# Edge messages of a graph network on one core: 42-wide one-hots, three accumulated row products, another order of steps, another beginning and close

## The chip, the cores and the metric

The kernel runs on one NeuronCore of a Trainium2 chip. The metric is device time in microseconds. Five engines work side by side, each through its own list in order, and wait for each other through semaphores: TensorE (PE), VectorE (DVE), ScalarE (ACT), GpSimd (POOL) and SyncE (SP), which here only starts transfers.

## The reference

A graph of 3125 nodes with 32 features each and 53125 edges (sorted by destination) goes through one layer. For every edge the features of its source and its destination are gathered, a small network of the edge's ten numbers gives weights, and the products are summed per edge; the edge outputs are summed over each destination, added to the features, and normalised.

```python
xs, xd = (x[edge_src], x[edge_dst])
s1 = concatenate([xs[:, :8], xd[:, :8]]); v1 = concatenate([xs[:, 8:], xd[:, 8:]])
w = _mlp(emb, fc1_w1, fc1_w2)            # E x 512
s_t = a1 * (einsum('eu,euw->ew', s1, Wss) + einsum('eu,euw->ew', vdot1, Wvv))
v_t = a1 * (einsum(s1, Wsv) * sh1 + einsum('euk,euw->ewk', v1, Wvs))
w2 = _mlp(emb, fc2_w1, fc2_w2)           # E x 384
edge_out = concatenate([tanh(scal), vecs * tanh(gates)]) * norm
x = _layernorm(x + segment_sum(edge_out, edge_dst, 3125))
```

## The kernel before

The edges lie in 104 blocks (`NB`) of 512 (`BE`), four tiles of 128 each. A block's destinations lie within 42 (`WIN`) consecutive nodes, counted from a base per block.

Every engine runs the same loop over `STEPS`, from -5 to 106. In step i an engine works on several blocks at once: step i has the main products of block i, the first layer of block i+1, the turned features of block i+2, the destination rows of block i+3, the turned one-hot of block i+4, and the late work (gates, tanh, sums over nodes) of blocks i-1 to i-3. The order of the work is that of the calls in each engine's loop, written by hand; nothing else schedules it.

For a block, in the order of its life:

- POOL gathers the sources' rows into `xs` by four indirect transfers (`gather`, L311), two blocks ahead of their use.
- DVE makes the one-hot of the destinations (`one_hot`, L520), bf16. It is 126 wide: 42 places, three times over, since the features `x` are stored in DRAM as three bf16 parts whose sum is the float32 value. PE turns it with four transposes (`turn_one_hot`, L708) and ACT copies the result to `oht` (`copy_oht`, L410).
- SP loads the block's 42 rows of all three parts into `window`, 126 partitions (`load_window`, L247). PE multiplies `oht` by `window` (`rows`, L752): four products, each contracting over 126 rows at once, so that the three parts are summed inside one product. ACT copies the rows into `fe` (`copy_rows`, L435).
- POOL makes the directed features from `fe` (`directions`, L351 to L357). PE turns `fe` (`turn_features`, L715), ACT copies it to `f` (`copy_f`, L416).
- PE makes the two hidden layers (`hidden`, L773 and L774) and multiplies `f` by the first weights (`first_layer`, L782). DVE multiplies by the hidden layer (`products`, L580), PE repeats and sums (`repeat`, L740), DVE multiplies again (`products2`, L603), PE sums (`sum_2`, L724) and turns (`turn`, L762), DVE and ACT make the outputs, PE sums them over the block's nodes (`over_nodes`, L732), DVE adds them to `acc`.

A wait that matters below: `rows(m)` waits until `copy_f` of block m-1 is done, for both use bank 4 of PSUM; ACT's list has `copy_oht` ahead of `copy_f`. `first_layer(m)` waits for both of DVE's instructions of `products2(m-1)`.

Before the loop stands the beginning: all inputs are loaded, `x` is split in three parts and stored to DRAM (`x_dram`), the first twelve blocks of edge attributes likewise (`e_dram`), the directions `r4` of all edges are normalised on DVE in one go, the constants and weights are made, and `acc` is zeroed on POOL. After the loop stands the close: the nodes' own features are multiplied by a centring matrix (L827) and the sums likewise (L833), and the norm is taken.

Of the kernel before, what the change touches and what calls it, by code (L numbers as in the profile page):

```python
# [7 lines left out]
BF16 = mybir.dt.bfloat16  # L8
# [7 lines left out]
D = 32  # L16
# [8 lines left out]
WK = PARTS * WIN  # L25
# [7 lines left out]
CHUNK = 32 * NT  # L33
HALVES = ((0, 13), (13, NT))
# [8 lines left out]
def program(nc, xp, xt, src_t, dst_t, base_t, bases_row, emb, vec_t, wgt, w1, w2a, w2b, out):  # L43
    ctx = ExitStack()
    with ctx:
# [9 lines left out]
        ones = sb("ones", [128, 1])  # L55
        iota_i = sb("iota_i", [128, P], I32)
        iota = sb("iota", [128, P])
        rank_i = sb("rank_i", [128, PARTS, WIN], I32)
        rank = sb("rank", [128, WK], BF16)
# [6 lines left out]
        no_rows = sb("no_rows", [WIN, PARTS, D], BF16)  # L66
# [13 lines left out]
        x_dram = nc.dram_tensor("x_dram", (PARTS, N + WIN, D), BF16, kind="Internal").ap()  # L80
# [3 lines left out]
        window_r = [sb(f"window{n}", [WK, D], BF16) for n in range(3)]  # L84
        oh_r = [sb(f"oh{n}", [128, T, WK], BF16) for n in range(OH)]
        oht_r = [sb(f"oht{n}", [WK, BE], BF16) for n in range(2)]
# [34 lines left out]
        x_part = early(P, PARTS * NT * D // 2).bitcast(BF16).rearrange("p (n m c) -> p n m c", n=PARTS, m=NT)  # L121
# [29 lines left out]
        oht_ps = ps[0:WK, 6, :].bitcast(BF16)[:, 0:BE]  # L151
# [17 lines left out]
        misfits_ready = sem("misfits_ready")  # L169
        n2_ready = sem("n2_ready")  # L170
        norm_ready = sem("norm_ready")
# [70 lines left out]
        def _(sp):  # L242
            def load_window(m):
# [3 lines left out]
                sp.dma_start(window_r[m % 3][:], x_dram[:, bass.ds(base, WIN), :]).then_inc(window_loaded[m % 3], 16)  # L247
# [21 lines left out]
            sp.dma_start(src_i[:], src_t).then_inc(src_loaded, 16)  # L269
            sp.dma_start(xt_s, xp.rearrange("(p m) c -> p m c", p=P)).then_inc(xt_loaded, 16)  # L270
            sp.dma_start(dst_i[:], dst_t).then_inc(dst_loaded, 16)
            sp.dma_start(base_i[:], base_t).then_inc(dst_loaded, 16)
            sp.dma_start(bases[:], bases_row).then_inc(bases_loaded, 16)
            load_super(0)
            sp.wait_ge(zeroed, 1)
            sp.dma_start(x_dram[:, N:N + WIN, :].rearrange("n m c -> m n c"), no_rows[:]).then_inc(x_stored, 16)
            for n in range(PARTS):
                sp.wait_ge(x_part_ready, n + 1)
                sp.dma_start(x_dram[n, 0:N, :].rearrange("(p m) c -> p m c", p=P), x_part[:, n, :, :]).then_inc(x_stored, 16)
            sp.wait_ge(bases_loaded, 16)  # L280
            sp.wait_ge(x_stored, 64)
# [608 lines left out]
```

## Time and profile before

| | us |
|---|---|
| median of three runs | 899.51 (896.36 to 900.3) |
| the profiled execution | 897.27 |
| its span | 895.4 |
| PE busy | 793.5 (89%) |
| DVE busy | 737.8 (82%) |
| POOL busy | 593.1 (66%) |
| ACT busy | 382.9 (43%) |

The profile's own execution is 1.87 us longer than its span, and 2.24 us shorter than the median. Busy time is an average over the whole span. What sets the pace is read from the order of time inside one step: who starts when, and who waited for whom. The timeline's rows give start, length, engine, line and operation; in brackets stands how long the engine was idle before, and what ended that. A row with xN merges N instructions: its length reaches from the first start to the last end. Ends of matmuls are modelled, starts are recorded; so the distance between two starts on PE is the safer number. A float32 product is two records on PE.

### The profile page before, as it was taken

The numbers are of one execution on the slowest core, as the hardware profiler recorded it, in microseconds if no ns is written. First come the engines' busy times: TensorE is split into PE (matmuls) and PEld (weight loads), VectorE is DVE, ScalarE is ACT, GpSimd is POOL, SyncE is SP. The second block draws the span as 40 slices with busy tenths as digits, with TensorE's granted clock in tenths as the row PEclk, the third lists the DMA queues.
The fourth block names the chain that finished last, engine by engine and source line by source line (L and its number), as shares of the span: only waits on it lengthen the run. The fifth ranks groups of instructions, "written<-read, shape, count | busy, mean of one in ns | idle before, by whom it ended". The sixth has DMA issues, their size and how long they took to land.

```text
span 895.4 us, 16890 instructions
## 1 busy us (share of the span) xinstructions
PE 793.5 (89%) x5234; PEld 362.1 (40%) x5234; DVE 737.8 (82%) x1397; ACT 382.9 (43%) x965; POOL 593.1 (66%) x866
## 2 busy tenths in 40 slices
PE   0179999999999999999999999999999999999983
PEld 0134444444444444444444444444444444444430
DVE  5648888888888888888888888888888888888873
ACT  3134444444445444444444444444454444444421
POOL 4877766677667667776677666767676667766300
PEclk9999999999999999999999999999999999999996
DMA  5111101111111111010111111111110110100000
GB/s 146 41 32 23 39 21 28 28 40 22 23 32 27 34 24 34 22 38 21 34 23 40 23 31 22 39 24 22 34 36 22 23 30 22 36 21 21 17 1 18
DMA packets 43733, 27.10 MB, mean 30 GB/s; under 512 B 21852, under 2 KB 42221, under 8 KB 43642
## 3 DMA queue, kind: packets, MB, share of 16 engines
q1 hardware_dynamic: 29498, 17.64, 7.5%
q0 software_dynamic: 13312, 6.84, 4.4%
q10 hardware_dynamic: 832, 1.52, 0.6%
q8 instruction: 42, 0.69, 0.3%
q14 instruction: 49, 0.40, 0.1%
HBM read 21.77 MB, written 4.20 MB: 29 GB/s over the span
## 4 chain that ended last, share of the span: by engine, by line
PE 78%; ACT 8%; issue 7%; DVE 3%; DMA 1%; POOL 1%; SPq 0%; ACTq 0%; DVEq 0%; POOLq 0%
PE ps L740 40%; PE ps L782 13%; PE ps L724 10%; PE ps L762 7%; ACT f L416 7%; PE ps L752 3%; PE ps L708 3%; PE ps L732 3%; DMA e_in<-in_emb 1%; DVE z_s L603 0%; POOL xs L311 0%; DVE w_f L569 0%; ACT oht L410 0%; PE ps L827 0%; PE ps L833 0%
## 5 line engine op out<-in xcount | busy, mean ns | idle before, releaser
L311 POOL DMA_INDIRECT xs<-in_xp,src_i x416 | 398.6, 958 | 110.4 <-issue 95.6
L740 PE MATMUL ps<-p_s,rep_m 128*128 128x512 f32 x832 | 374.5, 593 | 1.7 <-DVE p_s L580 1.7
L580 DVE TENSOR_TENSOR p_s<-ps,h 128x1024 f32<-128x1024 f32 x208 | 244.9, 1219 | 75.7 <-PE ps L782 75.7
L603 DVE TENSOR_TENSOR z_s<-ps,h 128x1024 f32<-128x1024 f32 x208 | 253.5, 1219 | 50.4 <-PE ps L740 50.2
L740 PEld LDWEIGHTS ps<-p_s,rep_m 128*128 128x128 f32 x832 | 150.0, 190 | 153.4 <-issue 149.2
L351 POOL TENSOR_TENSOR along<-fe,r 128x192 f32<-128x192 f32 x104 | 53.5, 514 | 127.1 <-issue 121.1
L410 ACT COPY oht<-ps 126x512 bf16<-126x512 bf16 x104 | 60.9, 586 | 177.6 <-PE ps L708 177.6
L422 ACT COPY u<-ps 128x512 f32<-128x512 f32 x104 | 61.0, 587 | 146.8 <-PE ps L724 146.8
L782 PE MATMUL ps<-f,w_f 32*128 32x512 f32 x832 | 119.5, 644 | 1.3 <-DVE z_s L603 1.3
L724 PE MATMUL ps<-z_s,w_z 128*32 128x512 f32 x832 | 108.0, 591 | 0.0
L404 ACT ACTIVATE eo_all<-gsc 128x64 f32<-128x64 f32 x104 | 26.7, 256 | 146.4 <-DVE gsc L618 144.9
L762 PEld LDWEIGHTS ps<-ident,u 128*128 128x128 f32 x416 | 43.8, 142 | 86.4 <-issue 86.3
L520 DVE TENSOR_TENSOR oh<-rank,place 128x504 bf16<-128x504 bf16 x104 | 70.1, 677 | 0.1
L708 PEld LDWEIGHTS ps<-ident_h,oh 128*126 128x126 bf16 x416 | 40.7, 140 | 70.2 <-issue 68.6
L715 PE MATMUL ps<-ident,fe 128*128 128x128 f32 x416 | 64.0, 277 | 5.1 <-POOL fe L357 5.1
L762 PE MATMUL ps<-ident,u 128*128 128x128 f32 x416 | 68.4, 287 | 0.0
L416 ACT COPY f<-ps 128x512 f32<-128x512 f32 x104 | 61.5, 591 | 9.7 <-PE ps L715 9.7
L448 ACT ACTIVATE h<-ps 128x512 f32<-128x512 f32 x104 | 63.9, 615 | 1.5 <-PE ps L773 1.5
L452 ACT ACTIVATE h<-ps 128x512 f32<-128x512 f32 x104 | 64.0, 616 | 0.0
L752 PE MATMUL ps<-window,oht 126*128 126x32 bf16 x416 | 26.2, 177 | 38.9 <-ACT f L416 38.9
L708 PE MATMUL ps<-ident_h,oh 128*126 128x128 bf16 x416 | 41.8, 224 | 16.7 <-DVE oh L520 15.3
L752 PEld LDWEIGHTS ps<-window,oht 126*128 126x128 bf16 x416 | 18.7, 96 | 87.1 <-issue 87.1
(96 smaller groups left out, 766.0 us busy)
## 6 DMA issues: line engine op xcount, KB each, us to landing
emb<-e_dram SPq DMA_DIRECT2D x312, 30.0 KB
xs<-in_xp,src_i POOLq DMA_INDIRECT x416, 2.3
e_dram<-e_part SPq DMA_DIRECT2D x8, 360.0 KB
e_in<-in_emb SPq DMA_DIRECT2D x8, 240.0 KB, 3.0
window<-x_dram SPq DMA_DIRECT2D x104, 7.9 KB
eo_all<-in_vec_t ACTq DMA_DIRECT2D x1, 624.0 KB, 4.8
x_dram<-eo_all SPq DMA_DIRECT2D x3, 195.3 KB
xt_n<-in_xt ACTq DMA_DIRECT2D x1, 400.0 KB, 10.3
```

What stands on the lines that cost most here:

```text
L311: nc.gpsimd.indirect_dma_start(xs_r[n][:, t, :], None, xp, bass.IndirectOffsetOnAxis(src_i[:, m * T + t:m * T + t + 1], axis=0)).then_inc( ...
L416: nc.scalar.copy(f_r[m % 2][:], f_ps).then_inc(f_copied, 1)
L452: nc.scalar.activation(h2_r[m % 3][:], h2_ps, ACT.Relu, scale=1.0 / math.sqrt(10.0)).then_inc(h2_ready, 1)
L520: nc.vector.tensor_tensor(oh_r[m % OH][:], rank[:].unsqueeze(1).to_broadcast([128, T, WK]), place[:, T * m:T * m + T].unsqueeze(2).to_broa ...
L580: nc.vector.tensor_tensor(p_s[:, a:a + 2, :], ps[:, a:a + 2, :], h1, ALU.mult).then_inc(p_done, 1)
L603: nc.vector.tensor_tensor(z_s[:, a:a + 2, :], ps[:, a:a + 2, :], h2, ALU.mult).then_inc(z_done, 1)
L708: last = nc.tensor.transpose(oht_ps[:, TE * t:TE * t + TE], oh_r[m % OH][:, t, :], ident_h[:])
L724: last = nc.tensor.matmul(s2_ps[32 * g:32 * g + 32], w_z[:, min(g, 1), :], z_s[:, g, :], start=True, stop=True)
L740: last = nc.tensor.matmul(ps[:, g, :], rep_m[:].rearrange("p j c -> p (j c)"), p_s[:, g, :], start=True, stop=True)
L752: last = nc.tensor.matmul(rows_ps[:, t, :], oht_r[m % 2][:, TE * t:TE * t + TE], window_r[m % 3][:], start=True, stop=True)
L762: last = nc.tensor.transpose(ps[:, 7, TE * t:TE * t + TE], u_r[k % 2][:, TE * t:TE * t + TE], ident[:])
L782: last = nc.tensor.matmul(ps[:, g, :], w_f[32 * g:32 * g + 32], f_r[m % 2][32 * g:32 * g + 32], start=True, stop=True)
```

## The change

It makes the one-hot 42 wide instead of 126, and stores the three parts of a node side by side (192 bytes in a row of `x_dram`). A window is then 42 partitions of three parts, and `rows` takes twelve products instead of four, three accumulated for each tile. PE and ACT take the features ahead of the one-hot (`turn_features` before `turn_one_hot`, `copy_f` before `copy_oht`). `over_nodes` also waits for `oht_copied`. `products2` has three instructions, over two, one and one of the four groups. The beginning loads and normalises the directions of the first 16 blocks (`CA`) alone; the rest is loaded after the first three windows, and DVE works on it between the one-hots of steps -3 to 5. The two subtractions that split `x` move from POOL to DVE. POOL starts to gather earlier, zeroes `acc` inside its loop in step -2, and has another order in steps below 1. PE's waits for weights and constants move from the loop's start to step -1. In the close, the product of the nodes' own features moves into step 105, and the table for the square root is loaded ahead of its use.

```diff
-        rank = sb("rank", [128, WK], BF16)
+        rank = sb("rank", [128, WIN], BF16)
-        x_dram = nc.dram_tensor("x_dram", (PARTS, N + WIN, D), BF16, kind="Internal").ap()
+        x_dram = nc.dram_tensor("x_dram", (N + WIN, PARTS * D), BF16, kind="Internal").ap()
-        oh_r = [sb(f"oh{n}", [128, T, WK], BF16) for n in range(OH)]
+        oh_r = [sb(f"oh{n}", [128, T, WIN], BF16) for n in range(OH)]
...
-            for m in range(3):
-                load_window(m)
-            store_super(0)
+            store_super(0)
+            sp.wait_ge(bases_loaded, 16)
+            sp.wait_ge(x_stored, 32)
+            load_window(0)
             sp.wait_ge(emb_zeroed, 3)
-            for m in range(3):
-                load_emb(m)
+            load_emb(0)
+            load_window(1)
+            load_emb(1)
+            load_window(2)
+            load_emb(2)
+            sp.dma_start(vt[:, TA:TILES, :], vec_t[:, TA:TILES, :]).then_inc(vect_loaded, 16)
+            sp.dma_start(src_i[:, TA:TILES], src_t[:, TA:TILES]).then_inc(src_loaded, 16)
+            sp.dma_start(wgt_s[:], wgt).then_inc(wgt_loaded, 16)
+            sp.dma_start(xt_n[:], xt).then_inc(nodes_loaded, 16)
...
             gather(0, 0, T)
-            gather(1, 0, T)
-            nc.gpsimd.memset(acc[:], 0.0).then_inc(acc_zeroed, 1)
+            rest_of_emb(0, 0)
+            gather(1, 0, 1)
+            rest_of_emb(0, 1)
+            gather(1, 1, T)
...
+                    if i < 1:
+                        if real(i + 3):
+                            directions(i + 3)
+                        if i == -2:
+                            nc.gpsimd.memset(acc[:], 0.0).then_inc(acc_zeroed, 1)
+                        if i + 4 >= 2:
+                            gather(i + 4, 0, T)
+                        if i == 0:
+                            gather(5, 0, T)
...
+                if real(i + 2):
+                    copy_f(i + 2)
                 if real(i + 4):
                     copy_oht(i + 4)
-                if real(i + 2):
-                    copy_f(i + 2)
...
+            nc.scalar.activation(warmed[:], warm[:], ACT.Sqrt)
...
-            def products2(k, a):
-                h2 = h2_r[k % 3][:].unsqueeze(1).to_broadcast([128, 2, BE])
+            def products2(k, n):
+                a, b = ((0, 2), (2, 3), (3, 4))[n]
+                h2 = h2_r[k % 3][:].unsqueeze(1).to_broadcast([128, b - a, BE])
...
-                if real(i + 5):
+                if real(i + 5) and i + 5 >= 2:
                     one_hot(i + 5)
+
+                for step, at_step in enumerate((-3, -2, 0, 1, 2, 3, 4, 5)):
+                    if i == at_step:
+                        ...
+                        ins = directions(step, TA, TILES)
...
                 for t in range(T):
-                    last = nc.tensor.matmul(rows_ps[:, t, :], oht_r[m % 2][:, TE * t:TE * t + TE], window_r[m % 3][:],
-                                            start=True, stop=True)
+                    for n in range(PARTS):
+                        last = nc.tensor.matmul(rows_ps[:, t, :], oht_r[m % 2][:, TE * t:TE * t + TE],
+                                                window_r[m % 3][:, n, :], start=(n == 0), stop=(n == PARTS - 1))
...
             for i in STEPS:
+                if i == NB + 1:
+                    nodes_themselves()
...
+                if real(i + 2):
+                    turn_features(i + 2)
                 if real(i + 4):
                     turn_one_hot(i + 4)
-                if real(i + 2):
-                    turn_features(i + 2)
```

PE in step 2, from the end of `repeat` to the end of `first_layer`, before. `ident` is the identity, `oh` the one-hot, `fe` the features, `emb` the edge attributes.

```order
L740 MATMUL ps<-p_s,rep_m 128x512
L708 MATMUL ps<-ident_h,oh6 126x128 [waits oht_copied,oh_made]
L708 MATMUL ps<-ident_h,oh6 126x128 x3
L715 MATMUL ps<-ident,fe0 128x128 [waits along_done]
L715 MATMUL ps<-ident,fe0 128x128 x3
L773 MATMUL ps<-emb0,w_first 128x512 [waits e_free,u_ready,emb_loaded0]
L774 MATMUL ps<-emb0,w_first 128x512
L752 MATMUL ps<-window2,oht1 128x32 [waits f_copied,window_loaded2]
L752 MATMUL ps<-window2,oht1 128x32 x3
L782 MATMUL ps<-f1,w_f 128x512 [waits z_done]
L782 MATMUL ps<-f1,w_f 128x512 x3
```

The same stretch of PE after the change (its own line numbers).

```order
L814 MATMUL ps<-p_s,rep_m 128x512
L788 MATMUL ps<-ident,fe0 128x128 [waits along_done]
L788 MATMUL ps<-ident,fe0 128x128 x3
L781 MATMUL ps<-ident_h,oh6 42x128 [waits oht_copied,oh_made]
L781 MATMUL ps<-ident_h,oh6 42x128 x3
L848 MATMUL ps<-emb0,w_first 128x512 [waits e_free,u_ready,emb_loaded0]
L849 MATMUL ps<-emb0,w_first 128x512
L827 MATMUL ps<-window2,oht1 128x32 [waits f_copied,window_loaded2]
L827 MATMUL ps<-window2,oht1 128x32 x11
L857 MATMUL ps<-f1,w_f 128x512 [waits z_done]
L857 MATMUL ps<-f1,w_f 128x512 x3
```

The features are turned first, the one-hot's output has 42 rows, and the row products are twelve.

POOL's first two blocks of directions, before: `xs` rows are gathers of source rows, L351 starts a block's directions.

```order
L311 DMA xs<-in_xp,src_i 128x32 x3
L351 TENSOR_TENSOR along<-fe,r 128x192 [waits rows_final,rows_copied,fe_copied]
L352 TENSOR_TENSOR fe<-fe,r 128x4x3x16
L355 TENSOR_TENSOR pair<-along 128x64 [waits fe_step]
L357 TENSOR_TENSOR fe<-pair,along 128x4x16 [waits fe_step]
L311 DMA xs<-in_xp,src_i 128x32 x4
L351 TENSOR_TENSOR along<-fe,r 128x192 [waits rows_final,along_done,rows_copied,fe_copied]
```

The same place after the change, to the second gather.

```order
L368 TENSOR_TENSOR along<-fe,r 128x192 [waits rows_final,rows_copied,fe_copied]
L369 TENSOR_TENSOR fe<-fe,r 128x4x3x16
L372 TENSOR_TENSOR pair<-along 128x64 [waits fe_step]
L374 TENSOR_TENSOR fe<-pair,along 128x4x16 [waits fe_step]
L368 TENSOR_TENSOR along<-fe,r 128x192 [waits rows_final,along_done,rows_copied,fe_copied]
L369 TENSOR_TENSOR fe<-fe,r 128x4x3x16
L372 TENSOR_TENSOR pair<-along 128x64 [waits fe_step]
L374 TENSOR_TENSOR fe<-pair,along 128x4x16 [waits fe_step]
L412 MEMSET acc 128x3200
L326 DMA xs<-in_xp,src_i 128x32 x4
```

The directions of the first two blocks now stand side by side, and the zeroing of `acc` and block 2's gather behind them.

DVE between the weights and the first products, after the change; before, five one-hots stood here in a row.

```order
L550 TENSOR_TENSOR oh2<-rank,place 128x168
L562 TENSOR_TENSOR r4<-eo_all 128x352x3 [waits vect_loaded]
L550 TENSOR_TENSOR oh3<-rank,place 128x168
L564 TENSOR_REDUCE eo_all<-r4 128x352 [waits r4_step]
L550 TENSOR_TENSOR oh4<-rank,place 128x168
L636 TENSOR_TENSOR p_s<-ps,h1_0 128x1024 [waits h1_ready,g_done]
```

The fourth one-hot (`oh3`) stands behind an instruction that waits for a transfer.

## Rows read from the trace of the kernel before

**Rows 1.** Page, part 4: share of the span in the chain, by engine

```profile
PE 78%; ACT 8%; issue 7%; DVE 3%; DMA 1%; POOL 1%; SPq 0%; ACTq 0%; DVEq 0%; POOLq 0%
```

**Rows 2.** Chain in order of time: start us, us, what; two repeats 96 steps apart

```profile
76.94 3.44 PE ps L740 x8
...
835.33 3.44 PE ps L740 x8
```

**Rows 3.** Timeline of one step: start us, us, engine line op [idle before]

```profile
404.11 0.39 PE L708 MATMUL ps<-ident_h,oh 128*126 128x128 bf16 x4
...
404.31 1.23 DVE L603 TENSOR_TENSOR z_s<-ps,h 128x1024 f32<-128x1024 f32 x1 [0.47 <-PE ps L740]
404.34 0.60 PE L715 MATMUL ps<-ident,fe 128*128 128x128 f32 x4
...
405.00 0.38 PE L774 MATMUL ps<-emb,w_first 96*128 96x512 bf16 x1
405.02 0.59 ACT L416 COPY f<-ps 128x512 f32<-128x512 f32 x1
...
405.73 0.18 PEld L752 LDWEIGHTS ps<-window,oht 126*128 126x128 bf16 x4 [0.84 <-issue]
405.75 0.25 PE L752 MATMUL ps<-window,oht 126*128 126x32 bf16 x4 [0.38 <-ACT f L416]
...
405.94 1.14 PE L782 MATMUL ps<-f,w_f 32*128 32x512 f32 x8
```

**Rows 4.** Timeline of steps 100 and 101, without one-hots to turn

```profile
846.51 0.60 PE L715 MATMUL ps<-ident,fe 128*128 128x128 f32 x4
...
847.15 0.59 ACT L416 COPY f<-ps 128x512 f32<-128x512 f32 x1 [1.75 <-PE ps L715]
...
847.88 0.25 PE L752 MATMUL ps<-window,oht 126*128 126x32 bf16 x4 [0.33 <-ACT f L416]
...
855.61 1.14 PE L782 MATMUL ps<-f,w_f 32*128 32x512 f32 x8 [0.45 <-DVE z_s L603]
```

**Rows 5.** Groups of instructions by shape: busy us, mean ns of one, idle before

```profile
L708 PEld LDWEIGHTS ps<-ident_h,oh 128*126 128x126 bf16 x416 | 40.7, 140 | 70.2 <-issue 68.6 <-DVE oh L520 1.7
...
L752 PEld LDWEIGHTS ps<-window,oht 126*128 126x128 bf16 x416 | 18.7, 96 | 87.1 <-issue 87.1
```

**Rows 6.** Timeline of the beginning

```profile
12.13 7.36 SPq L279 DMA_DIRECT2D x_dram<-eo_all  x3
...
22.57 0.94 POOL L311 DMA_INDIRECT xs<-in_xp,src_i  x1 [0.30 <-issue]
23.74 5.13 SPq L247 DMA_DIRECT2D window<-x_dram  x3
...
31.81 2.78 POOL L377 MEMSET acc<- 128x3200 f32 x1
32.28 6.56 SPq L254 DMA_DIRECT2D emb<-e_dram  x9
...
39.30 0.53 POOL L351 TENSOR_TENSOR along<-fe,r 128x192 f32<-128x192 f32 x1
...
41.01 1.11 PE L715 MATMUL ps<-ident,fe 128*128 128x128 f32 x4 [1.26 <-POOL fe L357]
...
47.55 1.11 PE L715 MATMUL ps<-ident,fe 128*128 128x128 f32 x4 [3.88 <-POOL fe L357]
...
53.06 3.70 PE L740 MATMUL ps<-p_s,rep_m 128*128 128x512 f32 x8 [1.35 <-DVE p_s L580]
```

**Rows 7.** Timeline of the close

```profile
874.95 0.28 PE L732 MATMUL ps<-ohs,eo_all 128*32 128x42 f32 x8 [2.05 <-DVE eo_all L594]
...
879.05 2.89 PE L827 MATMUL ps<-xt_n,centre 32*32 32x400 f32 x16 [0.81 <-issue]
...
886.49 1.28 ACT L508 ACT_TABLE_LOAD   x1
```

**Rows 8.** Stretch of the close: length, busy times, then the granted clock

```profile
879.00:882.00 3.00, 2.95 (x20) 0.71 (x24) 0.00 (x0) 0.00 (x0) 0.00 (x0) 0.50 0.00 0
```

More of the change, by code:

```diff
@@ L309, in gather @@
                     pool.wait_ge(fe_copied, m - 3)
+                if first == 0 and m == CA:
+                    pool.wait_ge(src_loaded, 32)
                 for t in range(first, end):
@@ L366, in _ @@
                                     pattern=[[-1, 128]], channel_multiplier=1).then_inc(pool_consts, 1)
-            for n in range(2):
-                of = xt_s if n == 0 else x_rest
-                pool.wait_ge(x_part_ready, n + 1)
-                nc.gpsimd.tensor_tensor(x_rest, of, x_part[:, n, :, :], ALU.subtract).then_inc(x_rest_ready, 1)
-                rest_of_emb(0, n)
             for n in range(3):
@@ L382, in _ @@
                 for i in STEPS:
-                    if real(i + 5) and i + 5 >= 2:
-                        gather(i + 5, 0, T)
                     if real(i + 3):
@@ L480, in _ @@
                     act.wait_ge(x_rest_ready, n)
[L481 removed]
+                nc.scalar.copy(x_part[:, :, n, :], xt_s if n == 0 else x_rest).then_inc(x_part_ready, 1)
                 if n < 2:
                     part_of_emb(0, n)
[L484 to L485 removed]
             for i in STEPS:
@@ L534, in _ @@
+            for step in range(2, 7):
+                link(directions(step, 0, TA))
+            directions(7, 0, TA).then_inc(r4_ready, 1)
+            rest_of_x(0)
+            dve.wait_ge(dst_loaded, 32)
             link(nc.vector.tensor_copy(dst_f[:], dst_i[:]))
@@ L634, in _ @@
                 if real(i):
-                    products2(i, 0)
-                    products2(i, 2)
+                    for n in range(3):
+                        products2(i, n)
                 if real(i - 2):
                     outputs(i - 2)
-                if real(i + 5):
+                if real(i + 5) and i + 5 >= 2:
                     one_hot(i + 5)
+                for step, at_step in enumerate((-3, -2, 0, 1, 2, 3, 4, 5)):
+                    if i == at_step:
+                        if step >= 1 and step != 2:
+                            dve.wait_ge(r4_step, step if step < 2 else step - 1)
+                        ins = directions(step, TA, TILES)
+                        if step == 1:
+                            ins.then_inc(n2_ready, 1)
+                        elif step == 7:
+                            ins.then_inc(r4_ready, 1)
+                        else:
+                            ins.then_inc(r4_step, 1)
             flag = dve.value_load(misfits[0:1, 0:1], min_val=0, max_val=EP)
@@ L823, in _ @@
                 pe.nop()
-            pe.wait_ge(nodes_loaded, 16)
-            for h in range(2):
-                for g in range(4):
-                    nc.tensor.matmul(ps[32 * g:32 * g + 32, 2 + h, 0:CHUNK // 2], centre[32 * g:32 * g + 32],
-                                     xt_n[32 * g:32 * g + 32, h * CHUNK // 2:(h + 1) * CHUNK // 2], start=True, stop=False)
             pe.wait_ge(sums_ready, 1)
```

188 lines of the change are left out of this document (118 added, 70 removed).

## The prediction

> **What bounds the kernel now.** I read the page's chain first: 78% of it is PE [rows 1]. The chain in order of time then shows a loop of even steps. Two repeats 96 steps apart start at 76.94 and 835.33 [rows 2], so a step takes (835.33 - 76.94) / 96 = 7.90 us. Then I read the timeline of one step, to find where PE waits within it. The reader is to see one gap. PE turns the one-hot at 404.11, the features at 404.34, and starts its second hidden product at 405.00; that product streams for some 0.2, so PE has run out of work at about 405.2. The row products start at 405.75, after a wait for ACT's copy of the features, and `first_layer` follows at 405.94 [rows 3]. From the first transpose to the row products PE needs 1.64 us, of which some 1.11 is work. DVE waits in the same step (0.47 before its second `products2` instruction [rows 3]), so it isn't the bound. The rest of PE's step, from 405.94 on, isn't touched by the change.
>
> Outside the loop lie a beginning, up to the first repeat at 53.06 [rows 6], and a close of some 25 us, in which engines wait for each other one by one.
>
> **The steady step.** Two edits meet here, and pull in opposite ways.
>
> The first gives back. With the features turned ahead of the one-hot, the copy starts earlier. Step 100 of the kernel before has no one-hot to turn, and shows what then happens: features at 846.51, copy at 847.15, row products at 847.88 [rows 4], 1.37 us instead of 1.64. That is 0.27 less, if PE's own work fits into 1.37.
>
> The second costs. Eight more products per step stand in front of `first_layer`. Four weight loads with a mean of 0.096 [rows 5] fill 0.18 [rows 3], so they start (0.18 - 0.096) / 3 = 0.028 apart. The four products take 0.19 up to the next group. At 0.028 each, eight more make 0.22, and the group 0.41.
>
> There is a third item. The last of the four row products starts at 405.75 + 3 x 0.028 = 405.83, and `first_layer`, on another tiling of the array, 0.11 later [rows 3]: 0.08 to 0.09 more than the spacing inside the group. The change puts the one-hot's transposes on a tile of 64 columns and the row products on one of 64 rows. Between the start of the features and that of the row products there are then three changes of tiling: work of 1.11 and three times 0.09 make 1.38, as much as the 1.37 that the copy needs. So the two paths tie.
>
> The Trainium skill ("TensorEngine Tiling (Array Packing)", Key Properties) says that a change of the tiling mode, not of the tile, drains TensorE. The 0.09 above agrees with it.
>
> The sum for a step: 1.38 + 0.41 against 1.64 + 0.19, or -0.04. Bounds: -0.09, if the products come every 0.024 and nothing else is late; +0.3, if each product costs the 0.058 of the one-hot's transposes ((404.34 - 404.11) / 4 [rows 3]), 0.24 more, and the drains some 0.05 besides. I take -0.04, since the nearest row is the same product with the same 128 stationary columns and 32 moving ones; only its depth falls from 126 to 42. There are 98 such steps (2 to 99): **-4 us**.
>
> The shorter one-hot on DVE (168 elements for 504) and the split of `products2` shorten an engine that waits for PE in these steps. They count for nothing there. The split matters where PE waits for `products2`: in the last three steps, where one wait is 0.45 [rows 4]. The last piece is then half as long as the 1.23 of now [rows 3], less an instruction's start: 0.4 each, **-1.2 us** together. ACT's copy of the one-hot comes behind the features' copy, and its later copies 0.2 later; the hidden layers are wanted only when `first_layer` is done, 1.1 after its start, so this hides.
>
> **The beginning.** Here `x` must arrive, be split in three, be stored, and come back as windows. Before, the first store is issued at 12.13, the third ends its issue at 19.49, and the first window starts at 23.74 [rows 6]: 4.25 behind it. The first store follows the arrival of `x` by one cast. Now `x` is first in SP's queue, and most of the directions, sources and edge weights, which shared the engines with it, come later. I estimate its arrival at 5.5 instead of 11. Bounds are 4 and 11. The chain of casts and subtractions keeps its 8 us, since the gather of block 0 now stands between two of them on POOL while the subtractions of `x` leave POOL. The single store then goes at 13.2, the first window at 17.7.
>
> SP now issues window and edge attributes by turns. Three windows take 5.13 and nine pieces 6.56 [rows 6]: 11.7 in all. So the late directions are asked for at 29.4 and arrive, by estimate, 4 later, at 33.4. This is an added wait: on DVE the fourth one-hot is behind it, and PE's `turn_one_hot(3)` behind that, ahead of the hidden layer and the first layer of block 0. With 1.5 for DVE's two instructions and 0.7 for the one-hot's way, and the 4.4 from the end of block 1's features (47.55 + 1.11) to the first repeat (53.06) [rows 6], step 0 starts at 40.0, 13 us earlier than now.
>
> But POOL can't keep up with that. A block's directions take 41.01 - 39.30 = 1.71, a gather of a tile 0.94 + 0.30 = 1.24, the zeroing 2.78 [rows 6]. Between the start of block 0's directions (21.3 by estimate: the window's landing and the row products) and the end of block 4's stand 5 directions, the zeroing, and 19 gathers: 8.6 + 2.8 + 23.6 = 35.0. Waits of some 5.5 for rows of blocks 1, 2 and 3 come on top: 61.8. PE turns these features at the end of step 2's repeat, now at 53.06 + 2 x 7.9 + 3.4 = 72.3. The gain is 10.5; with the table and queue waits that I can't see, I take **-10 us**. Bounds: -4, if `x` arrives as late as now, and -16, if POOL never waits. After that a step needs 4 x 1.24 + 1.71 = 6.7 of POOL, less than 7.9, so PE sets the pace again. The late pieces of the directions on DVE in steps 0 to 5 lie in its waits.
>
> **The close.** The nodes' product (2.89) stands between the last sum over nodes and the last product [rows 7]. It moves into step 105, where PE waits 2.05 for DVE [rows 7]. Its stretch ran at a granted clock of 0.50 [rows 8], the lower level of 1.2 GHz; PE was busy until a few us before, so in its new place it should run at 2.4 GHz in half the time, and fit into that wait: -2.8. The table (1.28 at 886.49 [rows 7]) goes, but DVE's reductions lie beside it, so about 0.4 of it counts. **-3.2 us**; bounds -2 (it runs at the low clock and delays step 105 by 0.9) and -4.6 (the last product keeps the high clock too).
>
> **The sum.** -4 - 1.2 - 10 - 3.2 = -18.4. On the profiled execution, 897.3, that is 878.9. This execution lies 2.2 below the median of the runs, 899.5, so the median I forecast is 881. Less than 0.5% (4.5 us) counts as no change.
>
> **The rivals.**
> - *The triple weight load becomes the bound.* Each of the twelve products loads its 128 columns anew. Three loads where one stood, at the 0.058 of the transposes, and drains that PE no longer hides, give +0.24 to +0.3 per step: 98 x 0.27 = +26 against -14.4 of the other parts, **+12: 911**, slower. It decides from 14.4 / 98 = +0.15 per step. For it: the one-hot's loads, bf16 too, have a mean of 0.140 [rows 5]. Against it: that is for 126 columns; the row products' loads with 128 columns, which stay, have 0.096 and come every 0.028.
> - *The beginning gains little.* The late directions arrive later still, or `x` does: -4 instead of -10, **887**. For it: twelve transfers stand ahead of it on SP. Against it: little else is moving then.
> - *The beginning gains all.* POOL waits for nothing and starts early, the last product keeps its clock: -16 and -4.6, **874**.
> - *The two halves cancel otherwise:* +0.13 per step, +13 instead of -4: **898**, no change.
>
> The Trainium skill ("TensorE: Matmul & The Clock Gate", LDWEIGHTS) gives a weight load as its columns divided by 1.2 in ns, whatever the depth; 128 columns make 107 ns. That speaks against this change, since a depth of 42 then buys nothing and eight more loads would cost 0.86 per step, 80 us in all. The spacing of 0.028 in this trace contradicts it for these loads. The same page (Weight-path perf modes) has faster loads for exactly 128 columns not in float32, which the trace bears out, and which the change keeps.
>
> **How the numbers follow.** The forecast has 0.58, the triple load 0.11, the small beginning 0.13, the large one 0.12, the cancelling 0.06. Faster: 0.58 + 0.13 + 0.12 = 0.83, and 0.01 of the cancelling: 0.84. Same: 0.05. Slower: 0.11. Its own range, from the unknown terms, is 872 to 889; to leave out no more than 2 in 10 over all cases, the range goes from 868 to 899, which takes in the small and the large beginning and part of the cancelling.
>
> **What would show it.** In the profile after: a step of 7.86 (7.8 to 7.9); row products that start 1.4 behind the features and take 0.4; the first repeat near 40, and features of block 4 turned near 62, released by POOL; DVE waiting for the directions' transfer before its fourth one-hot; the nodes' product in step 105 at the full clock. A step above 8.05 would make the forecast wrong, as would row products spaced by 0.05 or a first repeat after 48.

## The result, and the profile after

The changed kernel takes 892.96 us (median of 6 runs, 892.0 to 893.11) against 898.7 for the kernel before on the same chip (6 runs): ratio 0.9935, 95% interval 0.9921 to 0.995. It is 5.7 us, or 0.65%, faster; 18.5 us were forecast. The profiled execution took 892.88 with a span of 891.1, 4.3 less than the 895.4 of before.

The page's part 4 (share of the span in the chain, by engine) answers to [rows 1], and two repeats of the chain in order of time (start us, us, what), 96 steps apart, to [rows 2]:

```profile
PE 89%; DVE 2%; issue 0%; ACT 0%; DMA 0%; DVEq 0%; ACTq 0%
```

```profile
79.72 3.44 PE ps L814 x8
...
835.13 3.44 PE ps L814 x8
```

A step takes (835.13 - 79.72) / 96 = 7.87 us, 0.03 less than before. But the first of these repeats starts 2.8 *later* than its counterpart at 76.94, so the beginning gave nothing. The span is split by the starts of repeats (timeline; step 99 and the last were 835.17 and 865.80 before):

| stretch | before | after | difference | forecast |
|---|---|---|---|---|
| up to the repeat of step 4 | 84.67 | 87.42 | +2.75 | -10 |
| steps 4 to 99, 95 steps | 750.50 | 747.55 | -2.95 | -4 |
| step 99 to the last repeat | 30.63 | 29.78 | -0.85 | -1.2 |
| last repeat to the end | 29.6 | 26.35 | -3.25 | -3.2 |

**One step,** from its timeline (start us, us, engine line op, idle before), answers to [rows 3]:

```profile
405.77 0.60 PE L788 MATMUL ps<-ident,fe 128*128 128x128 f32 x4
...
406.30 0.40 PE L781 MATMUL ps<-ident_h,oh 128*42 128x128 bf16 x4
...
406.41 0.58 ACT L442 COPY f<-ps 128x512 f32<-128x512 f32 x1 [1.75 <-PE ps L788]
...
406.63 0.39 PE L848 MATMUL ps<-emb,w_first 96*128 96x512 bf16 x1
...
406.86 0.38 PE L849 MATMUL ps<-emb,w_first 96*128 96x512 bf16 x1
...
407.17 0.36 PEld L827 LDWEIGHTS ps<-window,oht 42*128 42x128 bf16 x12 [0.42 <-issue]
407.17 0.46 PE L827 MATMUL ps<-window,oht 42*128 42x32 bf16 x12
...
407.56 1.14 PE L857 MATMUL ps<-f,w_f 32*128 32x512 f32 x8
```

From the features to the row products there are 1.40, with no wait noted before the products; the twelve take 0.39 up to `first_layer` (L857): 1.79 against the 1.83 of before. ACT's copy of the features ends at 406.99, ahead of the row products at 407.17, so PE's own work sets this stretch now. The group of all 1248 weight loads of the row products (busy us, mean ns of one, idle before) answers to [rows 5]:

```profile
L827 PEld LDWEIGHTS ps<-window,oht 42*128 42x128 bf16 x1248 | 37.8, 93 | 57.0 <-issue 47.2 <-DMA window<-x_dram 9.8
```

**The beginning,** answering to [rows 6]. First the way of `x` (ACT L509 casts it, L488 casts the edge embeddings, L454 copies gathered rows, SP L285 stores `x`, L252 loads windows, L297 loads the late directions):

```profile
7.68 0.86 ACT L509 CAST eo_all<-eo_all 125x800 bf16<-125x800 f32 x1 [1.39 <-DMA eo_all<-in_xp]
...
14.13 1.16 POOL L346 TENSOR_TENSOR e_rest<-e_in,e_part 120x512 f32<-120x512 f32 x1
15.33 0.62 ACT L488 CAST e_part<-e_rest 120x512 bf16<-120x512 f32 x1 [4.87 <-POOL e_rest L346]
...
15.85 0.85 ACT L509 CAST eo_all<-eo_all 125x800 bf16<-125x800 f32 x1
...
16.73 0.29 SPq L285 DMA_DIRECT2D x_dram<-eo_all  x1
...
25.44 0.40 SPq L252 DMA_DIRECT2D window<-x_dram  x1
...
27.93 0.51 POOL L368 TENSOR_TENSOR along<-fe,r 128x192 f32<-128x192 f32 x1 [6.67 <-ACT fe L461]
...
32.43 0.51 POOL L368 TENSOR_TENSOR along<-fe,r 128x192 f32<-128x192 f32 x1 [2.85 <-ACT fe L461]
```

`x` is there at 7.68, not 5.5. Its third cast stands behind a cast on ACT that waits 4.87 for POOL, whose `e_rest` stands behind the gather of block 0. So the store leaves at 16.73, and the first window starts 8.7 behind it instead of 4.25: at 25.44, where 17.7 was forecast. Then the first steps:

```profile
36.13 0.43 SPq L297 DMA_DIRECT2D eo_all<-in_vec_t  x1
...
41.17 1.26 DVE L562 TENSOR_TENSOR r<-eo_all 128x1056 f32<-128x1056 f32 x1 [20.19 <-DMA eo_all<-in_vec_t]
...
42.72 0.62 PE L781 MATMUL ps<-ident_h,oh 128*42 128x128 bf16 x4 [7.47 <-DVE oh L550]
...
44.15 0.30 ACT L454 COPY fe<-xs 128x128 f32<-128x128 f32 x1 [11.85 <-DMA xs<-in_xp,src_i]
...
46.66 0.51 POOL L368 TENSOR_TENSOR along<-fe,r 128x192 f32<-128x192 f32 x1 [4.98 <-issue]
...
48.46 0.98 POOL L326 DMA_INDIRECT xs<-in_xp,src_i  x1
48.92 6.37 PE L814 MATMUL ps<-p_s,rep_m 128*128 128x512 f32 x8 [1.35 <-DVE p_s L636]
...
54.64 0.30 ACT L454 COPY fe<-xs 128x128 f32<-128x128 f32 x1 [7.72 <-DMA xs<-in_xp,src_i]
...
58.07 0.52 POOL L368 TENSOR_TENSOR along<-fe,r 128x192 f32<-128x192 f32 x1 [4.88 <-issue]
...
59.65 3.70 PE L814 MATMUL ps<-p_s,rep_m 128*128 128x512 f32 x8 [0.60 <-DVE p_s L636]
...
66.05 0.30 ACT L454 COPY fe<-xs 128x128 f32<-128x128 f32 x1 [6.34 <-DMA xs<-in_xp,src_i]
...
66.97 0.45 PE L827 MATMUL ps<-window,oht 42*128 42x32 bf16 x12 [2.31 <-ACT f L442]
...
71.50 3.60 PE L814 MATMUL ps<-p_s,rep_m 128*128 128x512 f32 x8
```

The reader is to see two things. The late directions hold DVE, and with it PE, until 42.7, as forecast, if later. And ACT waits three times for gathered rows, 11.85, 7.72 and 6.34, ahead of its copy of the features. This closes a loop: ACT waits for the gathered rows of a block; its copies behind that let PE make the block's destination rows; POOL turns these into its directions; and only behind them, in POOL's list, comes the gather of the next block. A turn that nothing else lengthens takes 10.4 us by estimate, where PE's own step is 7.9: 1.8 from block 3's directions (58.07) to the next block's gather (59.88), 6.2 until its rows are there (66.05), and 2.4 until ACT has copied the destination rows behind them (68.43). POOL's work isn't the bound in it: POOL waits 2.85, 4.98 and 4.88.

The loop doesn't decide each time. The wait of 7.72 cost nothing: the rows were there at 54.64, but PE came out of its first repeat, which is 6.37 long, only at 55.12, and ACT's copy of the features still waited 0.82 for PE. The wait of 6.34 did cost: PE had turned the features at 63.19 already, its row products waited 2.31 for ACT, and the third repeat came late.

The starts of the repeats split the +2.75. The first repeat comes 4.14 earlier than before. The second follows it after 10.73 instead of 7.86 (+2.87, the long first repeat), the third follows after 11.85 instead of 7.92 (+3.93, the gathered rows), and the next two add 0.09.

**The close,** answering to [rows 7] (timeline), and two stretches with the granted clock third from the end, answering to [rows 8]:

```profile
864.75 3.60 PE L814 MATMUL ps<-p_s,rep_m 128*128 128x512 f32 x8
...
871.36 1.55 PE L870 MATMUL ps<-xt_n,centre 32*32 32x400 f32 x16
...
877.98 2.89 PE L916 MATMUL ps<-acc,centre 128*32 128x400 f32 x16 [1.11 <-DVEq L738]
```

```profile
871.00:873.00 2.00, 1.91 (x20) 0.59 (x18) 1.21 (x6) 1.13 (x4) 0.00 (x0) 1.00 0.02 4
878.00:881.00 3.00, 2.87 (x16) 0.57 (x16) 0.06 (x1) 0.00 (x0) 0.00 (x0) 0.50 0.00 0
```

The nodes' product runs in step 105 at a granted clock of 1.00, the full 2.4 GHz, in 1.55; the last product, behind a wait, at 0.50, the lower level of 1.2 GHz, in 2.89, as before. The table for the square root is loaded at 875.87, ahead of its use.

### The profile page after: what moved, and what is told of

It reads as the page before. It is cut to its first block, busy times and chain, and to the rows that moved or that the text cites. A ratio compares the mean times of both kernels' runs of the same rounds, so it can differ in the third digit from the quotient of the medians.

```text
span 891.1 us, 18776 instructions
## 1 busy us (share of the span) xinstructions
PE 832.3 (93%) x6066; PEld 376.9 (42%) x6066; DVE 698.2 (78%) x1512; ACT 377.6 (42%) x967; POOL 589.3 (66%) x864
## 4 chain that ended last, share of the span: by engine, by line
PE 89%; DVE 2%; issue 0%; ACT 0%; DMA 0%; DVEq 0%; ACTq 0%
PE ps L814 39%; PE ps L857 12%; PE ps L797 10%; PE ps L837 7%; PE ps L788 5%; PE ps L827 4%; PE ps L781 4%; PE ps L848 4%; PE ps L806 2%; PE ps L849 2%; DVE z_s L666 1%; DVE p_s L636 0%; PE ps L916 0%; DMA xs<-in_xp,src_i 0%; DVE m L675 0%
## 5 line engine op out<-in xcount | busy, mean ns | idle before, releaser
L666 DVE TENSOR_TENSOR z_s<-ps,h 128x512 f32<-128x512 f32 (+1 forms) x312 | 250.7, 856 | 5.0 <-PE ps L814 5.0
L857 PE MATMUL ps<-f,w_f 32*128 32x512 f32 x832 | 119.9, 646 | 0.4 <-DVE z_s L666 0.4
L788 PEld LDWEIGHTS ps<-ident,fe 128*128 128x128 f32 x416 | 52.5, 143 | 58.6 <-issue 53.3
L781 PE MATMUL ps<-ident_h,oh 128*42 128x128 bf16 x416 | 42.6, 226 | 23.0 <-DVE oh L550 19.8
L474 ACT ACTIVATE h<-ps 128x512 f32<-128x512 f32 x104 | 61.6, 592 | 1.5 <-PE ps L848 1.5
L827 PEld LDWEIGHTS ps<-window,oht 42*128 42x128 bf16 x1248 | 37.8, 93 | 57.0 <-issue 47.2
L478 ACT ACTIVATE h<-ps 128x512 f32<-128x512 f32 x104 | 60.7, 584 | 0.0
L436 ACT COPY oht<-ps 42x512 bf16<-42x512 bf16 x104 | 60.0, 577 | 0.6 <-PE ps L781 0.6
L827 PE MATMUL ps<-window,oht 42*128 42x32 bf16 x1248 | 48.1, 174 | 12.7 <-DMA window<-x_dram 9.1
L369 POOL TENSOR_TENSOR fe<-fe,r 128x192 f32<-128x192 f32 x104 | 53.4, 513 | 0.0
```

The source lines that it names most:

```text
L474: nc.scalar.activation(h1_r[m % 2][:], h1_ps, ACT.Relu, scale=1.0 / math.sqrt(10.0)).then_inc(h1_ready, 1)
L666: nc.vector.tensor_tensor(z_s[:, a:b, :], ps[:, a:b, :], h2, ALU.mult).then_inc(z_done, 1)
L781: last = nc.tensor.transpose(oht_ps[:, TE * t:TE * t + TE], oh_r[m % OH][:, t, :], ident_h[:])
L788: last = nc.tensor.transpose(f_ps[:, TE * t:TE * t + TE], fe_r[m % 2][:, t].rearrange("p g c -> p (g c)"), ident[:])
L827: last = nc.tensor.matmul(rows_ps[:, t, :], oht_r[m % 2][:, TE * t:TE * t + TE], window_r[m % 3][:, n, :], start=(n == 0), stop=(n == PART ...
L857: last = nc.tensor.matmul(ps[:, g, :], w_f[32 * g:32 * g + 32], f_r[m % 2][32 * g:32 * g + 32], start=True, stop=True)
```

## The experiments: which part of the beginning

**Late directions on DVE moved to later steps** (changed kernel with):

```diff
-                for step, at_step in enumerate((-3, -2, 0, 1, 2, 3, 4, 5)):
+                for step, at_step in enumerate((0, 1, 3, 4, 5, 6, 7, 8)):
```

and ACT's square root of them from step -1 to step 2.

> The changed kernel, with DVE's work on the late directions (steps -3 to 5) moved to steps 0 to 8, so that no one-hot stands behind the wait for their transfer. Theory (the wait decides the beginning): the fourth one-hot is made near 21 us instead of 42, block 2's directions start on POOL at 42 instead of 46.7 and block 3's wait of 4.9 us goes; block 4's features are turned near 66 instead of 75; 9 us less than the changed kernel, about 884. Rival (POOL's own list decides, the wait lies beside it): the features of block 4 come at most 2 us earlier, about 891.

893.52 (ratio to before 0.9946, interval 0.9924 to 0.9968): no gain, the rival was right. Its timeline shows why. No one-hot waits for the directions any more, but the first repeat comes only 0.9 earlier (47.98), because ACT still waits for the gather:

```profile
43.21 0.30 ACT L454 COPY fe<-xs 128x128 f32<-128x128 f32 x1 [11.21 <-DMA xs<-in_xp,src_i]
```

**The gathers as in the kernel before.** On POOL, from block 2 on, the gather of block i+5 instead of i+4 stands around the directions of block i+3, two blocks ahead again, and `acc` is zeroed ahead of the loop (changed kernel with):

```diff
+            nc.gpsimd.memset(acc[:], 0.0).then_inc(acc_zeroed, 1)
...
-                        if real(i + 3):
-                            directions(i + 3)
...
-                        if i + 4 >= 2:
-                            gather(i + 4, 0, T)
...
+                    if real(i + 5) and i + 5 >= 2:
+                        gather(i + 5, 0, 3)
+                    if real(i + 3):
+                        directions(i + 3)
...
```

> The changed kernel with POOL's list as in the kernel before from block 2 on (three gathers of block i+5 ahead of the directions of block i+3), and acc zeroed before the loop, where POOL waits for the window. Theory (with a lead of one block, ACT's copy of the gathered rows blocks its copy of the features, that blocks the row products and POOL's next directions, a loop of 11 us or more per block): the waits of ACT for gathered rows of 11.8, 7.7 and 6.3 us go, step 2's repeat starts near 66 instead of 71.7, about 887. The late directions still hold the fourth one-hot until 42.5. Rival (POOL's sum of work decides, not its order): under 2 us, about 892.

886.73 (0.9861, 0.9842 to 0.9881), 6.2 below the changed kernel: the theory is right. The first repeat comes at 48.40, held by the directions now, and is as long as it was (6.35). So the second still comes 10.71 behind it, but the third follows that after 7.89 instead of 11.85:

```profile
59.11 3.70 PE L803 MATMUL ps<-p_s,rep_m 128*128 128x512 f32 x8 [0.60 <-DVE p_s L625]
...
67.00 3.63 PE L803 MATMUL ps<-p_s,rep_m 128*128 128x512 f32 x8
```

This bears out the reading above: the short lead of the gathers held PE once, in front of the third repeat.

**Both edits together:**

> The same, and DVE's late directions moved to steps 0 to 8. Theory (two waits in parallel: each hides the other, so that neither alone gives much): step 0's repeat starts near 42 instead of 48.9, step 2's near 61 instead of 71.7; 11 us less than the changed kernel, about 882, more than the two gains apart (0 and 6). Rival (the gains only add): about 887.

882.33 (0.9817, 0.98 to 0.9834), 10.6 below: the theory is right. Alone, moving the directions gave nothing; on top of the other it gives 4.4. The two waits ran side by side until 42 to 44 us, and each hid what the other's removal would have brought. The first repeats are now at 43.04, 52.94 and 60.83. The late directions aren't free in their new place, though: in step 3 DVE's reciprocal of them (2.35, from 73.67) stands ahead of the next products, and the repeat of step 4 comes 8.43 behind that of step 3 (77.15 against 68.72) instead of 7.87.

```profile
43.04 5.77 PE L803 MATMUL ps<-p_s,rep_m 128*128 128x512 f32 x8 [1.35 <-DVE p_s L625]
...
77.15 3.70 PE L803 MATMUL ps<-p_s,rep_m 128*128 128x512 f32 x8 [0.39 <-DVE p_s L625]
```

**The third cast of `x` ahead of the second of the embeddings** on ACT (changed kernel with):

```diff
-                if n < 2:
-                    part_of_emb(0, n)
+                if n == 0:
+                    part_of_emb(0, 0)
+            part_of_emb(0, 1)
```

> The changed kernel, with ACT's last cast of x ahead of its second cast of the edge attributes, which waits for POOL. Theory (x comes back late because its last cast stands behind POOL's gather of block 0): the store is issued near 13 us instead of 16.7, the first window and all behind it come 3.5 to 4 us earlier, about 889. Rival (the store itself is slow, or something later decides): the first window still starts after 24 us, and the time stays within 1 us of 893.

888.84 (0.9888, 0.9862 to 0.9914), 4.1 below: theory right. The store leaves at 13.07, the forecast's 13.2, and everything behind moves by 4. But the first window starts at 21.37, still 8.3 behind the store. So I also tried

**the same with the store in three transfers:**

```diff
-            sp.dma_start(x_dram[0:N, :].rearrange("(p m) c -> p m c", p=P), x_part.rearrange("p m n c -> p m (n c)")
-                         ).then_inc(x_stored, 16)
+            for lo, hi in ((0, 9), (9, 17), (17, NT)):
+                sp.dma_start(x_dram[0:N, :].rearrange("(p m) c -> p m c", p=P)[:, lo:hi, :],
+                             x_part[:, lo:hi].rearrange("p m n c -> p m (n c)")).then_inc(x_stored, 16)
```

> The changed kernel with the last copy of x ahead of the second embedding's, and the store of x in three transfers by range of nodes instead of one. With one transfer 8.3 us went from its issue at 13.07 to the first window at 21.37, and the time was 888.8. If one large transfer is slow because it is one: the first window near 18, the time near 885. Rival: the store is bound by its bytes, or by what it shares the engines with: the first window near 21 as before and the time within 1 us of 888.8.

889.0 (0.9893, 0.9875 to 0.9911), the first window at 22.25: the rival. The store isn't slow for being one transfer. In the kernel before, two of its three stores were on their way while the third part was still computed. A run below with that kernel's beginning and a single store (the narrow one-hot alone) issues it at 19.17 and loads the first window at 26.88, 7.7 behind, which bears this out. Whether bytes or the gathers beside them set the 6.9 to 7.7 that the one store takes to land wasn't tested.

**Everything together** (gathers ahead, directions later, `x` first, and the zeroing of `acc` on DVE), narrow:

> The same beginning as the wide kernel of this comparison, with the changed kernel's 42-wide one-hot and three row products. If x's earlier store adds to the two edits of the beginning (882.3 with them alone): 878 or so, 0.25 us a step or 24 to 26 us above the wide one. Rival: the store isn't on the path any more with both waits gone: 882.

881.89 (0.9819, 0.9801 to 0.9836), the same as the version without `x` first (ratio 0.9817): the rival's 882. In the profiles the step-4 repeat starts 1.3 earlier (75.85 to 77.15), so little of the 4 us from `x` is left once both waits are gone. Its chain in order of time shows what is late instead: it no longer goes through the store, as it did in the version without `x` first, but through POOL's gathers, from the arrival of the sources on:

```profile
1.20 7.18 DMA src_i<-in_src_t
8.66 1.14 POOL xs L326
...
33.30 0.94 POOL xs L326
34.26 0.53 POOL along L368
```

## The experiments: the step and the close

**The order alone** (kernel before with features turned and copied ahead of the one-hot, and one wait that keeps the windows' buffers safe):

```diff
-                if real(i + 4):
-                    turn_one_hot(i + 4)
                 if real(i + 2):
                     turn_features(i + 2)
+                if real(i + 4):
+                    turn_one_hot(i + 4)
...
```

> The kernel before, with features ahead of the one-hot on PE and ACT (and the one wait that this needs), nothing else. Theory: -0.27 per step as in step 100 of the kernel before, which has no one-hot to turn: 7.63, about 873 (-26). Rival: DVE's second products2 instruction, undivided here, ends too late for first_layer, and the step stops at 7.75 or more, about 885.

871.46 (0.9698, 0.9665 to 0.9731), 26 faster than the kernel before: the theory is right, and the undivided `products2` didn't hold the steady step. **The narrow one-hot alone** (kernel before with `WIN` for `WK` in one-hot and window, and):

```diff
-                    last = nc.tensor.matmul(rows_ps[:, t, :], oht_r[m % 2][:, TE * t:TE * t + TE], window_r[m % 3][:],
-                                            start=True, stop=True)
+                    for n in range(PARTS):
+                        last = nc.tensor.matmul(rows_ps[:, t, :], oht_r[m % 2][:, TE * t:TE * t + TE],
+                                                window_r[m % 3][:, n, :], start=(n == 0), stop=(n == PARTS - 1))
```

> The kernel before with the 42-wide one-hot, the new layout of x_dram and three row products per tile, its own order kept. Theory (each of the eight more products costs 0.025, and two more changes of tiling stand ahead of the copy of the features): the features are turned 0.09 + 0.23 + 0.09 behind the repeat instead of 0.23, the row products take 0.39 instead of 0.19; 8.28 us per step, +0.38, about 935. Rival (only the products cost, the changes of tiling hide): +0.20 per step, about 918.

938.52 (1.0447, 1.0429 to 1.0465), 40 slower: the theory is right. **The changed kernel with the 126-wide one-hot** and one row product per tile (the reverse of the last diff):

> The changed kernel with the one-hot 126 wide again and one row product per tile, all else kept. Theory (the three-fold products and the two more changes of tiling take back what the new order gives): the step falls from 7.87 to 7.63 us (row products take 0.19 instead of 0.39 and start 1.37 behind the features), 98 steps make -24, about 869. Rival (the step is bound elsewhere once the wait is gone, by DVE with its 0.35 us longer one-hot): the step stays above 7.8, about 890.

871.26 (0.9691, 0.9664 to 0.9717), 22 below the changed kernel: the theory is right. The steady step of the four:

| | one-hot first | features first |
|---|---|---|
| 126 wide, one product | 7.90 | 7.62 |
| 42 wide, three products | 8.30 | 7.87 |

The order gives 0.28 with the wide one-hot. The narrow one takes 0.25 of it back in the new order, and 0.40 in the old. PE's timelines show where. The order alone:

```profile
401.34 0.60 PE L715 MATMUL ps<-ident,fe 128*128 128x128 f32 x4
401.77 0.39 PE L708 MATMUL ps<-ident_h,oh 128*126 128x128 bf16 x4
...
402.70 0.25 PE L753 MATMUL ps<-window,oht 126*128 126x32 bf16 x4
402.88 1.14 PE L783 MATMUL ps<-f,w_f 32*128 32x512 f32 x8
```

and the narrow one alone:

```profile
406.85 0.40 PE L708 MATMUL ps<-ident_h,oh 128*42 128x128 bf16 x4
407.19 0.66 PE L715 MATMUL ps<-ident,fe 128*128 128x128 f32 x4
...
408.61 0.45 PE L753 MATMUL ps<-window,oht 42*128 42x32 bf16 x12 [0.33 <-ACT f L416]
408.99 1.14 PE L783 MATMUL ps<-f,w_f 32*128 32x512 f32 x8
```

In the first the row products start 1.36 behind the features, as they do in the changed kernel (1.40), and take 0.18. In the second the one-hot's transposes take 0.34 up to the features where the wide ones took 0.23 [rows 3]. They push the features' copy back by that, and the row products take 0.38: together 0.30 of the 0.40. The rest lies ahead of the transposes: they start 3.53 behind the start of the repeat in this run and 3.44 in the kernel before.

**Full tiles with the narrow form** (changed kernel; one-hot, its turned form and the windows padded with zeros from 42 to 66 places, still twelve products):

```diff
+WP = 66
-        window_r = [sb(f"window{n}", [WIN, PARTS, D], BF16) for n in range(3)]
-        oh_r = [sb(f"oh{n}", [128, T, WIN], BF16) for n in range(OH)]
-        oht_r = [sb(f"oht{n}", [WIN, BE], BF16) for n in range(2)]
+        window_r = [sb(f"window{n}", [WP, PARTS, D], BF16) for n in range(3)]
+        oh_r = [sb(f"oh{n}", [128, T, WP], BF16) for n in range(OH)]
+        oht_r = [sb(f"oht{n}", [WP, BE], BF16) for n in range(2)]
...
```

> The changed kernel with the one-hot, its turned copy and the windows padded with zeros to 66 places, so that transposes and row products use the whole array as before the change, with twelve products still. Theory (the eight more products are the cost, the changes of tiling lie beside the copy of the features): the row products start 1.37 behind the features instead of 1.40 and take 0.39; 7.84 per step, about 890. Rival (the drains are the cost): the step falls below 7.75, about 880.

887.66 (0.988, 0.9863 to 0.9896), a step of 7.82: the theory is right. PE in one step:

```profile
401.92 0.60 PE L790 MATMUL ps<-ident,fe 128*128 128x128 f32 x4
402.35 0.39 PE L783 MATMUL ps<-ident_h,oh 128*66 128x128 bf16 x4
402.58 0.38 PE L850 MATMUL ps<-emb,w_first 96*128 96x512 bf16 x1
...
403.28 0.45 PE L829 MATMUL ps<-window,oht 66*128 66x32 bf16 x12
403.67 1.14 PE L859 MATMUL ps<-f,w_f 32*128 32x512 f32 x8
```

So the tilings of the array account for 0.05 of the 0.25, and the eight further products for the other 0.20, 0.025 each. From one group's start to the next, the features take 0.43 here and the one-hot's transposes 0.23, where the changed kernel has 0.53 and 0.33: each change of tiling costs 0.10. Most of that lies beside ACT's copy, which lets the row products start 1.36 behind the features here and 1.40 there. The rule of the Trainium skill ("TensorEngine Tiling (Array Packing)", Key Properties) that a change of tiling mode drains TensorE agrees with these 0.10.

**The close alone** (kernel before with the nodes' product in step 105 and the table loaded ahead):

```diff
+                if i == NB + 1:
+                    pe.wait_ge(nodes_loaded, 16)
+                    for h in range(2):
+                        for g in range(4):
+                            nc.tensor.matmul(ps[32 * g:32 * g + 32, 2 + h, 0:CHUNK // 2], centre[32 * g:32 * g + 32],
...
```

> Before, with two edits of the close alone: the nodes' product in step 105, and ScalarE's square-root table loaded early. If the close is worth by itself what the two traces show together (29.6 us from the last repeat to the end before, 26.35 after), the time is 3.2 us below before's (about 895.5). Rival: the changed kernel's close is shorter only because its last steps hand their rows over earlier; then the two edits give less than 1.5 us (above 897).

896.59 (0.9979, 0.9964 to 0.9995), -1.9 with an interval from -3.2 to -0.4: between the two, and inconclusive by the time alone. The profile is clearer. From the last repeat to the last product it takes 13.56 where before took 16.07 (-2.5; 13.23 in the changed kernel). DVE's chain behind the product, from its first to its last `yn`, takes 4.00 instead of 4.42: the table's 0.4. The other way, this execution's beginning was 1.2 longer, with a first repeat of 5.25 instead of 3.70, and its last transfer 0.5 longer.

**The version that the runs point to** (wide one-hot and one product, in the changed kernel's order, with the four edits of the beginning):

> The changed kernel with the 126-wide one-hot and its single row product, GpSimd's gathers of two blocks ahead as before, the late directions on VectorE spread over the steps from 0 on, and the last copy of x ahead of the second embedding's. If the gains add: wide 871.3, less 10.6 for the two edits of the beginning (892.9 to 882.3 in the narrow kernel), less 4 or less for x: 856 to 861. Rival: with the beginning shorter a further wait for the gathered rows takes the place of those removed, and x gives nothing more: 861 to 866.

859.78 (857.17 to 860.18, 4 runs; ratio 0.9562, 0.9542 to 0.9581): 4.4% faster than the kernel before, and 22 below the same kernel with the narrow one-hot. It lies inside the theory's 856 to 861, but 11.5 below the wide kernel: the 10.6 of the two edits, and some 0.9 for `x` first and `acc` on DVE. Its first repeats start at 42.85, 53.37 and 61.01, and a step takes 7.62. The step from 3 to 4 takes 8.78, again behind DVE's reciprocal of the late directions, so some 1.2 us more may be had there, by estimate; no run tried it.

## Why the prediction was wrong

The direction was right, faster, but 5.7 of the 18.5 came; the time was 12 above the forecast, inside the range. By its own steps:

- **The steady step, -4: right.** 7.87 against 7.86; row products 1.40 behind the features (1.38) that take 0.39 (0.41). Loads of 128 columns with a depth of 42 have a mean of 93 ns and still come every 0.024 ((0.36 - 0.093) / 11). The three changes of tiling that it counted, at 0.09 each, are there: PE's groups from the features to the row products start 0.53, 0.33, 0.23 and 0.31 apart, where without such a change they need 0.43, 0.23, 0.22 and 0.22. The prediction's estimate that the order alone is worth 0.27 was also right (0.28). The rival of the triple weight load fell, and with it what the Trainium skill's LDWEIGHTS section ("TensorE: Matmul & The Clock Gate") would make of it, 107 ns for each load: the trace, with 12 loads in 0.36, decides against it here.
- **The last steps, -1.2: right,** -0.85. The last two steps are 0.50 shorter each; the one before is 0.19 longer, since its row products are twelve now too. The split of `products2` is what shortens them: with features first and the wide one-hot, the last step takes 7.55 undivided (the order alone) and 7.05 divided (the changed kernel with the wide one-hot). Forecast were 0.4 in each of three.
- **The close, -3.2: right,** -3.25, by the mechanism given: 1.55 at the full clock in step 105, the last product at the lower level.
- **The beginning, -10: this step failed,** at +2.75. The prediction let POOL start block 0's directions at 21.3, added 35.0 of its work up to the end of block 4's, and "waits of some 5.5 for rows of blocks 1, 2 and 3": 61.8. Measured were a start at 27.93, some 34.4 of work, and waits of 2.85, 4.98 and 4.88, 12.7 together: 75.1. So the work was right, the start 6.6 too early, and the waits 7.2 too short. The waits were put at too little because their structure was missed: between two blocks POOL doesn't just wait for rows; the rows wait for ACT, ACT for the gather, and the gather for POOL's directions before. That the changed list puts each gather behind the directions was read, but what stands behind the waiting instruction on ACT was not asked. Restoring the lead gives 6.2, and moving the directions 4.4 on top. One of the three waits, the 4.88, was not the loop's: it is the long first repeat, which the prediction had no term for.
- The 6.6 lie ahead of that: the estimate "at 13.2 the single store goes, the first window at 17.7" was off by 3.5 and 7.7. The 3.5 is a cast of another stream in front of the third cast (13.07 without it). The arrival of `x` at 7.68 instead of 5.5 added nothing to it, since the casts and subtractions took 5.3 (7.80 to 13.07) instead of 8 in that run. The distance from store to window, taken over from a store that ended a pipeline of three, gave 4.5.
- DVE waiting for the late directions was forecast with its place. It came 7.8 late (41.17 against 33.4), yet removing it alone gave nothing.

The forecast said a first repeat after 48 would show it wrong; it came at 48.92. With both waits removed the beginning is 7.5 us shorter than before at step 4 (77.15 against 84.67), and 8.8 with `x` first and `acc` on DVE as well (75.85), near the -10. The forecast was that of a kernel without these waits. The +2.75 itself has luck in it: the profiled execution of the kernel before had a first repeat of only 3.70, where the close alone, which keeps its beginning, had 5.25 and the order alone 5.55.

## What to carry to other kernels

Where every engine works through its list in order, a transfer's lead, counted in blocks, can matter more than the work of the engine that issues it. Follow each wait around until it comes back to the engine it started from: that loop, not the engine's sum, can be the least time per block. Then ask of each wait in it what else ended at the same time: of the three here, one cost 3.9 us, one nothing, and one hid behind a second wait until both were removed. And split a change that bundles a gain and a loss in the same stretch: here one line's order was worth 0.28 a step, and the narrower one-hot beside it cost 0.25.

## What was not expected of the hardware

- The first repeat, eight products of 128x512 in float32, took 3.70 in the profile of the kernel before and 6.37 in the changed kernel, with products of up to 1.22 in place of 0.59. In the other versions it took 5.12 to 6.64. The granted clock is shown as 1.00 there, so only the durations tell it. What PE did before isn't shown to be the cause: the changed kernel's PE had stood still from 35.25 to 42.72, but the version with the close alone, whose PE does the same short pieces from 35.90 on as the kernel before (36.24), had 5.25. The cause stays open.
- The depth of a weight load didn't matter: 93 ns with 42 rows, 96 with 126 [rows 5], and 0.024 to 0.028 from one load to the next.
- The 586 KB store of `x` took 6.9 us to land (from 13.07, in the chain of the best version), and 7.7 from 16.91 in the version with both edits. In three pieces it let the first window start no earlier (22.25 against 21.37).
